# Maxima rows in the last quarter of the contraction rows, written by ScalarE; key blocks without fills; third query amid the first maxima

## The chip, the core and the metric

The kernel runs on one core of a Trainium2 chip. TensorE (PE) multiplies matrices from on-chip memory into PSUM, VectorE (DVE) reduces and combines, ScalarE (ACT) evaluates functions and copies, GpSimd (POOL) does small elementwise work, and SyncE (SP) issues most DMA transfers. Each engine works through its own queue in order and waits on semaphores. The metric is the time of one execution in microseconds (us), the median of several.

## The reference

Two layers act on x (4 batches, 512 positions, 128 channels) with a context of 154 keys per batch:

- Layer 0: x += tanh(g) * attention(layernorm(x), ctx), 16 heads of 8 channels, softmax over 154 keys. Then x += tanh(g) * FFN(layernorm(x)), a feed-forward part with activations rounded to 16 bits and weights to 4 bits.
- Layer 1: the same attention with its own weights and much larger keys, then a recurrent cell of four steps over the batches, which ends in a tanh.

What is computed for a head is softmax(q k / sqrt(8)) v for 512 queries and 154 keys. The kernel subtracts each query's largest score before the exponential; the masks of layer 1 only keep a tile's overlapping keys from counting twice.

## The kernel before

**Queries and key blocks.** `Q4` holds a batch's queries for scores with 128 contraction rows: of every four rows (`PARTS = 4`) one is the query's high part, one its low part, one the high part again, and the fourth is a row for maxima. `Kd` holds for every group of four heads four blocks of 154 keys; block j has keys only in 32 of the 128 rows, the rest is zero. One matmul thus gives the scores of three or four heads, or, with `Kd` as the stationary operand, the transposed scores of one head. There are three buffers of each, used in turn by batch number n = 4 * layer + b. All zeros are written by fills: VectorE and GpSimd fill `Q4` and `Kd` (`clear`, `clear_rest`, `clear_early`, `clear_late`), then engines copy 32 rows a block (`diagonal`).

**Maxima.** First pass, per batch: `scores_for_top` computes the scores in units (22 in layer 0, 20 in layer 1) of up to four heads into one of three PSUM banks (`MRING`), and VectorE's `take_top` reduces each to negative maxima. `split_top` splits them in high and low parts (`nms`), TensorE's `turn_top` transposes them into the PSUM bank `misc`, ScalarE's `copy_top` copies 32 rows into `nmT`, and SP's `tops` writes them by two DMAs into the maxima rows of `Q4`. The second pass (`scores`, 16 tiles of 128 keys and 4 tail tiles) then gives scores less the maximum, ScalarE's `exps` turns each tile, and TensorE's `weigh` multiplies them with the values in rounds of four tiles.

**Order.** Loops over layer, iteration i = -1 to 4 and slot 0 to 19 set every engine's queue: in iteration i slot s, score tile s of batch i is computed, and maxima units of batch i+1 in slots 0 to 12. Iteration -1 is a prologue: only the maxima units of batch 0. Some units are taken early, in slots 17 to 19 of the iteration before: for batch 1 eight (`FIRST_EARLY`). All else stands in plans of (slot, what, shift): "pre" is the transposing of a normalised batch, "q" its projection to queries, "top" the turning of maxima, "post" the transposing after attention, "wo" the projection of the output. Shift 3 stands for the third query in the prologue, shift -1 for the previous batch. "pre", "q", "top", "post" and "wo" share the one bank `misc`; `fill_misc` makes TensorE wait until the previous user has been read, which for the maxima is `nmT_r`.

**GpSimd's queue in layer 0** is: fills, the root of the first two norms, more fills, the frames of ones in the values (`frames`), `biases`, `values`, `tail_keys`, and then, in the loop, the third batch's norm, its key block and its low query part.

Of the kernel before, what the change touches and what calls it, by code (L numbers as in the profile page):

```python
# [32 lines left out]
PARTS = 4  # L33
# [6 lines left out]
FIRST_EARLY = 8  # L40
# [58 lines left out]
PE_PLAN = [(1, "tail0", -1), (3, "tail1", -1), (4, "pre", 2), (18, "pre", 3), (6, "q", 2), (19, "q", 3), (7, "round0", 0), (8, "wo", -1),  # L99
# [5 lines left out]
ACT_PLAN = [(5, "pre", 2), (6, "q", 2), (14, "top", 1), (18, "pre", 3), (19, "q", 3), (16, "post", -1),  # L105
# [12 lines left out]
VALUES_AT = ((0, -1, 5), (0, -1, 9))  # L118

# [61 lines left out]
def program(nc, x, w, wkr, ctxT, tailT, wffn, cols, rows, consts, masks, out):  # L181
    with ExitStack() as ctx:  # L182
# [61 lines left out]
        with ExitStack() as stretch:  # L244
# [11 lines left out]
            nmT = sb_here("nmT", [32, 2, T], F32R)  # L256
# [13 lines left out]
            nil = sb_here("nil", [32, T])  # L270
# [39 lines left out]
        q4_clear, kd_clear, nil_r = sem("q4_clear"), sem("kd_clear"), sem("nil_r")  # L310
        zero_r = sem("zero_r")
# [10 lines left out]
        m_in = [sem(f"m_in{n}") for n in range(3)]  # L322
# [25 lines left out]
        def misc_read(name):  # L348
# [8 lines left out]
            if kind == "top":  # L357
                return nmT_r, B * name[1] + name[2] + 1
# [16 lines left out]
        def q_landed(n):  # L375

            return q_in[n % 3], 16 * sum(5 if m in CLEAN_MAX_ROWS else 3 for m in range(n % 3, n + 1, 3))

        def kd_cleared(layer, b):

            return kd_clear, 3 if (layer, b) == (1, 0) else 2 * layer + min(b, 2) + 1
# [3 lines left out]
        def _(sp):  # L385
# [13 lines left out]
            def queries(layer, b):  # L399
                n = B * layer + b  # L400
                sp.wait_ge(q4_clear, 3 * layer + min(b, 2) + 1)
                if n >= 3:
                    sp.wait_ge(score_r, TILES * (n - 2))
                for a, (src, ready) in enumerate(((qh, qh_r), (ql, ql_r), (qh, qh_r))):
                    sp.wait_ge(ready, n + 1)
                    sp.dma_start(Q4[n % 3][a:P:PARTS, :, :].bitcast(F32),
                                 src[:, n % 2, :].bitcast(F32)).then_inc(q_in[n % 3], 16)
                if n in CLEAN_MAX_ROWS:
                    sp.wait_ge(nil_r, 1)
                    for a in range(2):  # L410
# [1153 lines left out]
```

## Time and profile before

| | us |
|---|---|
| runs | 371.2, 370.77, 369.09 (median 370.77) |
| profiled execution | 368.43 |
| its span, first to last instruction | 366.2 |
| busy in the span | PE 290.1, DVE 250.3, ACT 193.0, POOL 127.5 |
| granted TensorE clock, mean | 0.925 |

Two attention phases (20 to 128 us and 221 to 325 us) enclose the feed-forward part; the recurrent cell lies at the end. In each attention phase iteration -1 ends with the first score tile (48.4 and 241.7 us), and iterations 0 to 3 follow. Busy shares are means over stages with different limits, so each stage is read by itself. A line such as "PE L914" is line 914 of the kernel; the bracket at the end of a line of the timeline is the engine's idle time before it and what released it.

### The profile page before, as it was taken

The numbers are of one execution on the slowest core, as the hardware profiler recorded it, in microseconds if no ns is written. First come the engines' busy times: TensorE is split into PE (matmuls) and PEld (weight loads), VectorE is DVE, ScalarE is ACT, GpSimd is POOL, SyncE is SP. The second block draws the span as 40 slices with busy tenths as digits, with TensorE's granted clock in tenths as the row PEclk, the third lists the DMA queues.
The fourth block names the chain that finished last, engine by engine and source line by source line (L and its number), as shares of the span: only waits on it lengthen the run. The fifth ranks groups of instructions, "written<-read, shape, count | busy, mean of one in ns | idle before, by whom it ended". The sixth has DMA issues, their size and how long they took to land. (4 is left out here: it accounts for less than half of the span.)

```text
span 366.2 us, 4506 instructions
## 1 busy us (share of the span) xinstructions
PE 290.1 (79%) x1459; PEld 171.7 (47%) x1459; DVE 250.3 (68%) x530; ACT 193.0 (53%) x302; POOL 127.5 (35%) x263
## 2 busy tenths in 40 slices
PE   0976299899998785996006888899999999999794
PEld 0554164454543243431005765575665755544444
DVE  4788364896963589789989968765685792415414
ACT  1635066466466734869689634056555547463122
POOL 6588870444050301780001069431165023030300
PEclk9989689999999999998556999599999999999989
DMA  8721020020000000000000011110001000000004
GB/s 218 278 83 61 9 86 4 5 93 7 2 8 0 3 0 0 3 0 0 1 0 0 0 61 55 61 70 23 9 37 63 2 0 10 0 2 0 1 0 116
DMA packets 9687, 12.56 MB, mean 34 GB/s; under 512 B 896, under 2 KB 5376, under 8 KB 9664
## 3 DMA queue, kind: packets, MB, share of 16 engines
q1 hardware_dynamic: 9232, 11.80, 9.0%
q10 hardware_dynamic: 432, 0.47, 0.7%
q8 instruction: 12, 0.20, 0.2%
q14 instruction: 11, 0.09, 0.1%
HBM read 4.27 MB, written 1.05 MB: 15 GB/s over the span
## 5 line engine op out<-in xcount | busy, mean ns | idle before, releaser
L1215 DVE TENSOR_REDUCE sb_nm<-ps_top 128x3 f32<-128x462 f32 (+2 forms) x168 | 97.3, 627 | 41.4 <-PE ps_top L900 25.9
L721 ACT ACTIVATE sb_pr<-ps_score 128x512 f32<-128x512 f32 (+1 forms) x160 | 89.7, 584 | 61.8 <-PE ps_score L931 28.0
L900 PE MATMUL ps_top<-sb_Kd,sb_Q 128*128 128x462 f32 (+3 forms) x240 | 73.7, 384 | 7.3 <-DVE sb_nm L1215 3.2
L928 PE MATMUL ps_score<-sb_Q,sb_Kd 128*128 128x512 f32 x128 | 59.6, 477 | 3.9 <-ACT sb_pr L721 3.9
L589 POOL TENSOR_SCALAR sb_var<-sb_mv 128x4 f32<-128x4 f32 x16 | 5.3, 333 | 147.7 <-DVE sb_mv L1178 147.5
L900 PEld LDWEIGHTS ps_top<-sb_Kd,sb_Q 128*128 128x128 f32 x240 | 44.8, 206 | 22.3 <-DVE sb_nm L1215 13.2
L928 PEld LDWEIGHTS ps_score<-sb_Q,sb_Kd 128*128 128x128 f32 x128 | 23.9, 190 | 40.3 <-ACT sb_pr L721 31.3
L960 PE MATMUL ps_pv<-sb_pr,sb_V 128*32 128x512 f32 x256 | 34.1, 605 | 0.0
L606 POOL TENSOR_SCALAR sb_xn<-sb_xr,sb_nmean,sb_rstd 128x128 f32<-128x128 f32 x48 | 21.2, 455 | 1.3
L877 PE MATMUL ps_misc<-sb_consts,sb_xn 128*128 128x128 f32 x64 | 11.3, 304 | 12.7 <-POOL sb_xn L606 11.1
L1235 DVE STREAM_TRANSPOSE sb_oq<-ps_pv 128x512 f32<-128x512 f32 x16 | 10.7, 696 | 13.3 <-PE ps_pv L960 13.3
L591 POOL TENSOR_TENSOR sb_rstd<-sb_var,sb_half 128x4 f32<-128x4 f32 x16 | 16.6, 1040 | 1.3
L491 POOL CAST sb_Kd<-sb_K 32x616 fp32r<-32x616 f32 x20 | 13.9, 694 | 8.5 <-ACT sb_front L810 7.5
L936 PE MATMUL ps_score<-sb_Q,sb_KT 128*128 128x512 f32 (+1 forms) x32 | 14.6, 472 | 1.7 <-ACT sb_pr L721 1.7
L960 PE MATMUL ps_pv<-sb_pr,sb_VT 128*32 128x512 f32 (+1 forms) x128 | 14.9, 550 | 0.9 <-ACT sb_pr L721 0.9
L877 PEld LDWEIGHTS ps_misc<-sb_consts,sb_xn 128*128 128x128 f32 x64 | 7.8, 155 | 16.2 <-POOL sb_xn L606 12.6
L1175 DVE BATCH_NORM_STATS2 sb_stat<-sb_xr 128x6 f32<-128x128 f32 x64 | 13.9, 279 | 1.4 <-DMA sb_xr<-x 1.1
L1016 PE MATMUL ps_misc<-sb_consts,sb_amx 128*128 128x128 f32 x10 | 2.9, 383 | 14.9 <-DVE sb_amx L1276 14.2
L693 ACT ACTIVATE sb_xnT<-ps_misc 128x512 f32<-128x512 f32 x8 | 4.8, 596 | 18.1 <-PE ps_misc L877 18.1
L931 PE MATMUL ps_score<-sb_maskr,sb_identr 128*128 128x128 f32 x64 | 14.2, 222 | 0.0
L904 PE MATMUL ps_top<-sb_maskr,sb_identr 128*128 128x512 f32 (+3 forms) x48 | 13.8, 289 | 0.0
L700 ACT ACTIVATE sb_qh<-ps_misc,sb_cols 128x512 fp32r<-128x512 f32 x8 | 5.5, 688 | 15.8 <-PE ps_misc L883 15.8
(167 smaller groups left out, 545.5 us busy)
## 6 DMA issues: line engine op xcount, KB each, us to landing
sb_Q<-sb_qh SPq DMA_DIRECT2D x16, 256.0 KB, 2.3
sb_Q<-sb_ql SPq DMA_DIRECT2D x8, 256.0 KB, 2.3
sb_xr<-x SPq DMA_DIRECT2D x4, 256.0 KB, 7.6
out<-sb_xr SPq DMA_DIRECT2D x4, 256.0 KB, 2.4
sb_wsb<-w SPq DMA_DIRECT2D x1, 704.0 KB, 8.4
sb_wf<-wffn SPq DMA_DIRECT2D x1, 576.0 KB, 8.2
sb_wkr<-wkr SPq DMA_DIRECT2D x2, 256.0 KB, 7.1
sb_Q<-sb_nmT SPq DMA_DIRECT2D x16, 32.0 KB
```

The lines of the kernel that those rows point to most:

```text
L491: ins = pool.tensor_copy(Kd[n % 3][q, :, j, :], K4[q, :, b, :])
L591: pool.tensor_tensor(rstd[:, k % 4, :], var[:, k % 4, :], half[:, :], ALU.pow).then_inc(rstd_r, 1)
L606: ins = pool.tensor_scalar(xn[:, kind == "post", t, :], xr[:, TT * b + t, :], nmean[:, k % 4, t:t + 1], rstd[:, k % 4, t:t + 1], ALU.add, ...
L721: act.activation(pr[:, k % PRING, q0:T], score[k % SRING][:, q0:T], ACT.Exp, scale=SCALE).then_inc(exp_r, 1)
L877: ins = pe.transpose(misc[:, P * t:P * t + P], xn[:, kind == "post", t, :], ident[:, :])
L900: ins = pe.matmul(cols[:, c0:c1, :], Q4[n % 3][:, g, P * qt:P * qt + P], Kd[n % 3][:, g, j:j + c1 - c0, 0:keys], start=True, stop=not mask ...
L928: ins = pe.matmul(ps[:, :], Kd[n % 3][:, g, j, 0:P], Q4[n % 3][:, g, :], start=True, stop=(layer == 0), skip_group_check=True)
L931: ins = pe.matmul(ps[:, 0:P], identr[:, :], maskT, start=False, stop=True, skip_group_check=True)
L936: ins = pe.matmul(ps[:, q0:T], KT[:, b, t - H, :], Q4[n % 3][:, t - H, q0:T], start=True, stop=(layer == 0), skip_group_check=True)
L960: ins = pe.matmul(acc[32 * g:32 * g + 32, q0:T], lhs, pr[:, (TILES * n + t) % PRING, q0:T], start=(r in (0, 2)), stop=(r >= 4), skip_group ...
L1175: ins = dve.bn_stats(stat6[:, k % 4, t, :], xr[:, TT * b + t, :])
L1215: dve.tensor_reduce(nm[:, :, :].rearrange("p t h -> p (t h)")[:, f0:f0 + heads], top[k % MRING][:, 0:keys * heads].rearrange("p (h k) -> p ...
```

## The change

- The contraction rows are laid out anew: rows 0 to 95 hold the three query parts (every third row), rows 96 to 127 the maxima. ScalarE writes these straight from `misc` into `Q4`, one copy for each of four groups of heads, two at slot 14 and two at slot 15; `nmT`, its two DMAs and SP's `tops` are gone. TensorE turns the maxima with matmuls against the identity instead of transposes.
- The zeros of the maxima rows, which the first pass needs, are written by one DMA per query from a tile of zeros. The low query part is issued last.
- Key blocks and tails are written over all 128 rows, as the keys times a column of ones and zeros (`block_of[j]`). All fills of `Q4`, `Kd` and `KT` are gone.
- The third query's "pre" and "q" in the prologues move from slots 18 and 19 to 8 and 11, and in layer 0 its norm on GpSimd moves ahead of `biases` and `values`.
- Batch 1's early units are three instead of eight, at slot 14 of iteration -1.
- ScalarE's copies of the values, its block of batch 1 and the masks of layer 0 move from ahead of the loop into slots 5 and 9, 6, and 16 of iteration -1.

```diff
-PARTS = 4
+PARTS = 3
+MAX0 = 96
-FIRST_EARLY = 8
+FIRST_EARLY = 3
+FIRST_EARLY_AT = 14
 def units_at(layer, i, slot):
-    if slot >= SLOTS - EARLY and 0 < i + 2 < B:
+    if (i, slot) == (-1, FIRST_EARLY_AT):
+        taken += [(1, u) for u in range(FIRST_EARLY)]
+    if slot >= SLOTS - EARLY and 1 < i + 2 < B:
-PE_PLAN = [..., (18, "pre", 3), ..., (19, "q", 3), ...
+PE_PLAN = [..., (8, "pre", 3), ..., (11, "q", 3), ...
-ACT_PLAN = [(5, "pre", 2), (6, "q", 2), (14, "top", 1), (18, "pre", 3), (19, "q", 3), (16, "post", -1),
+ACT_PLAN = [(5, "pre", 2), (6, "q", 2), (14, "top0", 1), (15, "top1", 1), (8, "pre", 3), (11, "q", 3), (16, "post", -1),
 def misc_read(name):
-                return nmT_r, B * name[1] + name[2] + 1
+                return nmT_r, G * (B * name[1] + name[2] + 1)
 def queries(layer, b):          # SP
+                sp.wait_ge(nil_r, 1)
...
+                sp.dma_start(Q4[n % 3][MAX0:P, :, :].bitcast(F32), nil[:, :, :].to_broadcast([32, G, T])).then_inc(q_in[n % 3], 16)
+                for a, src, ready in ((0, qh, qh_r), (2, qh, qh_r), (1, ql, ql_r)):
-            def tops(layer, b):
 def diagonal(layer, b):         # POOL; ACT and DVE alike
-                    ins = pool.tensor_copy(Kd[n % 3][q, :, j, :], K4[q, :, b, :])
+                    ins = pool.tensor_scalar(Kd[n % 3][:, :, j, :], K4[:, :, b, :].bitcast(F32), block_of[j], 1.0,
+                                             ALU.mult, ALU.mult)
                 if layer == 0:                                    # POOL's queue
-                    clear_rest()
                     frames()
+                    normed("pre", 0, 2)
                     biases()
                     values(0)
                     tail_keys(0)
-                else:
-                    clear_late()
-            def copy_top(layer, b):
+            def copy_top(layer, b, groups):
                 act.wait_ge(misc_full, use["top", layer, b] + 1)
-                act.activation(nmT[:, n % 2, :], misc[0:32, :], ACT.Copy).then_inc(nmT_r, 1)
+                for g in groups:
+                    act.activation(Q4[n % 3][MAX0:P, g, :], misc[MAX0:P, :], ACT.Copy).then_inc(nmT_r, 1)
 def turn_top(layer, b):         # PE
-                    ins = pe.transpose(misc[0:32, P * t:P * t + P],
+                    ins = pe.matmul(misc[MAX0:P, P * t:P * t + P], nms[:, t, :, :, :]...,
+                                    ident[:, :], start=True, stop=True)
 def scores(layer, b, t):        # PE
-                if t == 0:
-                    pe.wait_ge(m_in[n % 3], 2 * 16 * (n // 3 + 1))
+                if t < G:
+                    pe.wait_ge(nmT_r, G * n + t + 1)
```

## Rows read from the trace of the kernel before

**Rows 1.** Busy time by stage (iteration -1 in part, 0 and 1; then layer 1).
```profile
core 0: us, PE busy (x) PEld busy (x) DVE busy (x) ACT busy (x) POOL busy (x), PEclk, DMA share, GB/s
...
36.00:45.20 9.20, 2.60 (x9) 1.78 (x7) 2.82 (x5) 0.59 (x1) 7.86 (x22) 0.69 0.02 9
...
48.40:65.90 17.50, 16.13 (x85) 8.64 (x83) 9.80 (x19) 12.24 (x23) 4.62 (x9) 0.99 0.13 49
65.90:89.30 23.40, 21.55 (x123) 11.61 (x122) 19.36 (x49) 13.71 (x26) 11.98 (x23) 1.00 0.10 40
...
234.60:241.70 7.10, 7.05 (x29) 5.80 (x30) 4.41 (x7) 1.18 (x2) 0.00 (x0) 0.64 0.02 9
```

**Rows 2.** Timeline, end of layer 0's prologue (start us, length us, what).
```profile
34.74 0.31 ACT L747 ACTIVATE sb_identr<-sb_consts 128x128 fp32r<-128x128 f32 x1
34.89 0.28 DVE L1228 TENSOR_TENSOR sb_nms<-sb_nm,sb_nms 128x64 fp32r<-128x64 f32 x1
34.96 0.43 ACT L749 ACTIVATE sb_maskr<-sb_cmask 128x288 fp32r<-128x288 f32 x1
...
35.23 1.04 PE L914 MATMUL ps_misc<-sb_consts,sb_nms 128*32 128x128 f32 x4 [1.54 <-DVE sb_nms L1228]
...
36.30 0.59 ACT L712 ACTIVATE sb_nmT<-ps_misc 32x512 fp32r<-32x512 f32 x1 [0.91 <-PE ps_misc L914]
...
39.03 2.61 POOL L504 CAST sb_KT<-sb_K 32x512 fp32r<-32x512 f32 x4
...
43.46 1.74 POOL L606 TENSOR_SCALAR sb_xn<-sb_xr,sb_nmean,sb_rstd 128x128 f32<-128x128 f32 x4
...
45.25 1.12 PE L877 MATMUL ps_misc<-sb_consts,sb_xn 128*128 128x128 f32 x4 [6.64 <-POOL sb_xn L606]
...
50.26 4.64 ACT L721 ACTIVATE sb_pr<-ps_score 128x512 f32<-128x512 f32 x8
```

**Rows 3.** Timeline, ScalarE at the end of layer 1's prologue.
```profile
235.72 0.59 ACT L712 ACTIVATE sb_nmT<-ps_misc 32x512 fp32r<-32x512 f32 x1 [6.97 <-PE ps_misc L914]
...
243.50 1.09 ACT L721 ACTIVATE sb_pr<-ps_score 128x512 f32<-128x512 f32 x2
```

**Rows 4.** Timeline of TensorE: score 17 of iteration 0; the output's projection.
```profile
62.97 0.50 PE L936 MATMUL ps_score<-sb_Q,sb_KT 128*128 128x512 f32 x1 [0.45 <-ACT sb_pr L721]
...
77.86 1.05 PE L969 MATMUL ps_misc<-sb_wsb,sb_oT 128*128 128x128 f32 x8
```

**Rows 5.** Timeline, maxima and post norm at slots 14 to 16 of iteration 1.
```profile
84.66 0.61 PE L914 MATMUL ps_misc<-sb_consts,sb_nms 128*32 128x128 f32 x4
...
85.31 0.59 ACT L712 ACTIVATE sb_nmT<-ps_misc 32x512 fp32r<-32x512 f32 x1
...
85.80 1.05 ACT L721 ACTIVATE sb_pr<-ps_score 128x512 f32<-128x512 f32 x2
...
86.04 0.63 PE L877 MATMUL ps_misc<-sb_consts,sb_xn 128*128 128x128 f32 x4 [0.24 <-ACT sb_nmT L712]
```

**Rows 6.** The page's costliest groups (busy, mean ns) and DMA issues (KB, us to landing).
```profile
L1215 DVE TENSOR_REDUCE sb_nm<-ps_top 128x3 f32<-128x462 f32 (+2 forms) x168 | 97.3, 627 | 41.4 <-PE ps_top L900 25.9
...
L606 POOL TENSOR_SCALAR sb_xn<-sb_xr,sb_nmean,sb_rstd 128x128 f32<-128x128 f32 x48 | 21.2, 455 | 1.3
...
L491 POOL CAST sb_Kd<-sb_K 32x616 fp32r<-32x616 f32 x20 | 13.9, 694 | 8.5 <-ACT sb_front L810 7.5
...
sb_Q<-sb_qh SPq DMA_DIRECT2D x16, 256.0 KB, 2.3
```

**Rows 7.** Iteration 0 of layer 0, the matmuls of line 900 alone.
```profile
48.40:65.90 17.50, 6.32 (x26) 4.86 (x26) 0.99 0.13 49
```

**Rows 8.** Timeline of TensorE in the feed-forward part.
```profile
146.07 1.96 PE L1098 MATMUL ps_score<-sb_front,sb_wfT 128*128 128x512 f32 x4 [1.90 <-DVE sb_front L1365]
...
163.69 1.88 PE L1098 MATMUL ps_pv<-sb_front,sb_wfT 128*128 128x512 f32 x4
167.88 3.62 PE L1098 MATMUL ps_score<-sb_front,sb_wfT 128*128 128x512 f32 x4 [2.31 <-ACT sb_uf L777]
```

More of the change, by code:

```diff
@@ L118 @@
 VALUES_AT = ((0, -1, 5), (0, -1, 9))
+FIRST_DIAGONAL_AT = (0, -1, 6)
+MASKS_AT = (0, -1, 16)
 KRING = 4
@@ L211, in program @@
         lowrow = consts_sb[:, P + 1:P + 2]
+        block_of = [consts_sb[:, P + 2 + j:P + 3 + j] for j in range(J)]
         cmask = sb("cmask", [P, 2 * P + 32])
@@ L375, in q_landed @@
         def q_landed(n):
-            return q_in[n % 3], 16 * sum(5 if m in CLEAN_MAX_ROWS else 3 for m in range(n % 3, n + 1, 3))
-        def kd_cleared(layer, b):
-            return kd_clear, 3 if (layer, b) == (1, 0) else 2 * layer + min(b, 2) + 1
+            return q_in[n % 3], 16 * 4 * (n // 3 + 1)
         @block.sync
@@ L663, in copy_k, with copy_v @@
                                scale=lowrow).then_inc(kh_r, 1)
-            def copy_v(layer):
+            def copy_v(layer, kinds):
                 if layer == 1:
                     act.wait_ge(v_r, 1)
-                for t in range(2):
+                for t in kinds:
                     act.wait_ge(vmm, 2 * layer + t + 1)
@@ L1213, in take_top @@
                 f0, heads, keys = UNITS[layer][u]
+                if u == 0 and k > 0:
+                    dve.wait_ge(nms_r, B * layer + b)
                 dve.wait_ge(top_r, k + 1)
@@ L1510, in constants @@
     own = (a % 32 >= OWN)[:, None]
-    low = (a % PARTS == 2)[:, None]
-    return tuple(np.concatenate(parts, axis=1).astype(np.float32) for parts in ((ident, own, low), (top, main, tail)))
+    low = ((a < MAX0) & (a % PARTS == 2))[:, None]
+    head = np.where(a < MAX0, a // PARTS // D, a % H // G)[:, None] == np.arange(J)[None, :]
+    return tuple(np.concatenate(parts, axis=1).astype(np.float32) for parts in ((ident, own, low, head), (top, main, tail)))
 def kernel(**inputs):
@@ L1524 @@
         turned.append(t[:, order] if name.endswith("Wq") else t)
-    wkr = np.zeros((C, 2, G, J, 32), np.float32)
-    bkr = np.ones((J, 32, 2, G), np.float32)
+    wkr = np.zeros((C, 2, G, P), np.float32)
+    bkr = np.zeros((P, 2, G), np.float32)
+    for g in range(G):
+        bkr[MAX0 + g::G, :, g] = 1.0
     for n in range(2):
@@ L1532 @@
         for part in range(3):
-            wkr[:, n, :, :, part::PARTS] = wk
-            bkr[:, part::PARTS, n, :] = bk.transpose(1, 2, 0)
+            wkr[:, n, :, part:MAX0:PARTS] = wk.reshape(C, G, J * D)
+            bkr[part:MAX0:PARTS, n, :] = bk.transpose(1, 2, 0).reshape(J * D, G)
     ctx = np.asarray(inputs["ctx_1024"]).transpose(2, 0, 1)
```

120 lines of the change are left out of this document (44 added, 76 removed).

## The prediction

> **What bounds the kernel now.** I read the busy time by stage first [rows 1]. In the attention iterations TensorE is busy 16.13 of 17.5 us and 21.55 of 23.4 us: they are paced by TensorE with ScalarE and VectorE close behind, whatever waits there lengthens the kernel. The two places where TensorE waits are the prologues. From 36.0 to 45.2 us it is busy only 2.60 of 9.2 us. The timeline says why [rows 2]: the third query's transposes stand in TensorE's queue at slot 18 and wait 6.64 us for GpSimd, which first does the values, then the tail keys (2.61 us from 39.03) and only then the normalisation at 43.46. The maxima of batch 0 were split by 35.17 and copied by 36.89, yet the first exponential starts at 50.26. In layer 1 there is no such wait (234.6 to 241.7 us is full, at 0.64 of the clock), only eight early maxima units and the third query stand between the copy at 235.72 and the exponential at 243.50 [rows 3].
>
> **Prologue of layer 0.** Gone: all fills of Q and Kd, the tails' fill, and the place of the third query behind values and tail keys. GpSimd then normalises batch 2 right after the frames, before any value; TensorE takes its transposes at slot 8 and its projection at slot 11, among 22 reduces of VectorE that pace this stretch. I charge 0.3 us for them (0 if VectorE always has three units ahead, 1.2 if TensorE runs at half clock there). Maxima split: 35.17 + 0.3 = 35.5. Turning them is no transpose any more but an fp32 matmul, which is issued as two instructions; the projection of the output does the same four products in 1.05 us [rows 4], where four transposes took 0.61 at full clock [rows 5] and 1.04 at half [rows 2]. So 1.05 to 1.8 us, I take 1.4: 36.9. Then four ScalarE copies instead of one. Two ScalarE instructions of 512 columns start 0.49 apart (85.31 and 85.80) and the last runs 0.59 [rows 5]: 3 x 0.49 + 0.59 = 2.1, so 39.0. Identity and masks, moved behind them, are 0.31 + 0.43 us [rows 2]. First exponential at 39.8 instead of 50.26: **-10.5 us** (-9.5 to -11.5). Late next: the values on GpSimd. Their first copy moves only little, so they end near 37; round 0 wants them at slot 7, near 45. The DMAs that carried the maxima were hidden behind the same 6.64 us; taking them away gains nothing of its own.
>
> GpSimd's diagonals now write 128 rows by a tensor-scalar instead of copying 32. That operation at 616 columns is not in the trace: below it lies the copy of 616 columns, 0.694 us; above it the 128-column tensor-scalar of 0.455 us scaled by width, 2.19 us [rows 6]. I take 1.1, nearer the row of equal width: 4.4 us for a block instead of 2.96. In layer 0 the tail keys end near 41, the third block near 45.5, its low query lands near 49, and its first unit is wanted at slot 17, near 54. Nothing. The GPSIMD Engine Reference of the Trainium skill, section 3.1, gives one-input bodies of few operations about 1.03 cycles an element at 1.2 GHz; an estimate from it is the copy's price, with which this trace's copy agrees (0.694 us for 616 columns). By the page the block would cost no more than now and the sum would not move; only the last rival would lose its chance.
>
> SP's queue: for each query it issues one 256 KB zero DMA and three query parts instead of three parts (and two small ones twice), the zeros ahead of the query's wait, so they land while SP waits for the query. The low part is now last, three issues in either order. 0 us; if the zeros came late, one landing of 2.3 us [rows 6], once a layer. VectorE's and ScalarE's blocks keep their width in columns and so their time: 0.
>
> **Iteration 0 of both layers.** Batch 1's early units fall from eight to three, so five move out of the prologue into slots 0 to 12. In layer 0, TensorE's unit matmuls are 6.32 us for 14 units in this iteration [rows 7], 0.45 each or 2.3 for five, of which TensorE's idle time of 1.4 us takes little; below, 0.5 if ScalarE hides them, above, five reduces of 0.627 us [rows 6], 3.1. I take **+2.0 us**. In layer 1 the five carry masks: **+2.2 us** (1 to 3.4).
>
> **The maxima copies at slots 14 and 15.** This is the term that decides. Iteration 1 now: TensorE turns the maxima at 84.66, ScalarE copies at 85.31, does exponentials 15 and 16 from 85.80, and TensorE's next user of the same PSUM bank, the transposes of the post norm at slot 16, starts at 86.04, as soon as the copy ends at 85.90 [rows 5]. Both queues are in order. After: the matmuls end 0.45 later; ScalarE copies two groups (85.75, 86.24), does exponential 15 (86.73), copies the other two (87.22, 87.71), done at 88.30. The post transposes wait for all four copies, since they overwrite the bank: they start at 88.44 instead of 86.04, **+2.4 us**. Behind them in TensorE's queue stand score 17, round 3 and the next early units, behind those VectorE's reduces; nothing of it can start earlier. It holds for iterations 1 and 2 of both layers: 4 x 2.4 = **+9.6 us**. Bounds for each: 0.45 (all but the dearer matmuls regained) and 3.4 (one more us at low clock). In iteration 0 no post norm follows; there exponential 15 is behind two more copies, round 3 and score 17 (62.97 now [rows 4]) wait for it: 63.9, +0.95, and the later copies keep that: 2 x 0.95 = **+1.9 us**.
>
> **Prologue of layer 1.** The copy begins at 235.72, after 1.04 us of turning as in layer 0, so the maxima are split near 234.6. The third query among the reduces adds 0.4, and the third early unit, which needs the last reduce's buffer, stands before the turn: 235.9. At half clock 1.8 us of matmuls, to 237.7; then the copies; exponential at 239.6 instead of 243.50 [rows 3]: **-3.9 us** (-2.5 to -5). GpSimd's fills there delay nobody: TensorE has no idle time in that stretch [rows 1]. Both first iterations now begin out of stretches granted 0.69 and 0.64 on the mean, partly at 1.2 GHz, where iteration 0 of layer 0 had 0.99 [rows 1]: **+1.0 us** in all (0 to 2).
>
> **Sum.** -10.5 + 2.0 - 3.9 + 2.2 + 9.6 + 1.9 + 1.0 = +2.3 us. The profiled execution took 368.43 us (366.2 of span, 2.2 around it), so 370.7; the median of the runs is 370.77, 2.3 above the profiled one, so on the median's basis 373.1 us. A measurement here tells 0.5%, 1.9 us, from no change.
>
> **Rivals.** (B) *The delays at the copies are regained*: VectorE, not TensorE, would pace the following slots. For: it is busy 19.36 of 23.4 us of iteration 1, with only 4.0 us idle [rows 1]. Against: its reduces come from units that stand behind the blocked transposes. If each of the four costs 0.5 instead of 2.4, the sum is 2.3 - 7.6 = -5.3 and the time 370.77 - 5.3 = 365.5 us: faster. It decides from 1.1 us regained of each 2.4, where the sum passes -1.9.
> (C) *The clock falls at each copy stall.* TensorE would stand 2.1 us at slot 16, four times. After an idle of 2.31 us in the feed-forward part, four matmuls took 3.62 us where four just before took 1.88 [rows 8]: 1.8 us each time, +7.2: 380 us. Against: four after an idle of 1.90 us took 1.96, full clock [rows 8]. [...]
> (D) *The five moved units are free*: iteration 0 is paced by ScalarE (12.24 busy) and they slip beside it: 2.3 - 3.7 = -1.4, 369.4 us.
> (E) *The tensor-scalar is at its upper bound*: 8.8 us a block and, scaled likewise, 7.2 for tail keys puts the third block of layer 0 at 53 and the low query's landing near 57, so slot 17 waits 3 us, and again 3 in iteration 1: 379 us. That is also the case in which the change does not do what it says, for GpSimd would still hold the queue.
>
> **How the numbers follow.** Forecast 0.42, B 0.22, C 0.14, D 0.13, E 0.09. The forecast's own range, 370.5 to 376, comes from the bounds of its terms taken against each other; 0.24 of it is beyond +0.5%, 0.16 within, 0.02 below. B gives 0.20 faster and 0.02 same; D 0.06 faster, 0.07 same; C all slower; E 0.08 slower, 0.01 same. Together faster 0.28, same 0.26, slower 0.46. The range reaches from the middle of B to the middle of C, leaving out 0.11 and 0.07: 365.5 to 380.
>
> **What would show it.** TensorE's gap before 45 us gone, first exponential near 40 (and 240 less the shift in layer 1). Post transposes at slot 16 with an idle of about 2 us released by the copy into Q, four times; iteration 1 lasting about 25.8 instead of 23.4 us: if it stays at 23.4, B is right. Iteration 0 at 20 to 21 us instead of 17.5: if 18, D. Full-clock matmuls right after the stall exclude C. GpSimd's block near 4.4 us decides E. Wrong altogether would be a stage outside the prologues and slots 14 to 16 that moves by over 1 us.

## The result, and the profile after

| | before | changed |
|---|---|---|
| runs, us | 368.73 to 371.2, median 369.93 | 380.51, 383.31, 382.93, 378.34, median 381.72 |
| ratio, 95% interval | | 1.030 (1.025 to 1.035) |
| profiled execution, its span | 368.43, 366.2 | 380.51, 378.7 |
| busy PE, DVE, ACT, POOL | 290.1, 250.3, 193.0, 127.5 | 297.2, 248.7, 207.7, 108.5 |
| granted clock, mean | 0.925 | 0.913 |

The change makes the kernel 3.0% slower. The forecast was 373.1 us, with 380 as the upper end of its range; the measured 381.7 lies beyond it. Medians and ratios, here and below, leave out executions over 1.5% above a kernel's fastest; with them the medians of experiments 2 (both edits), 3 (three units), 7 (first) and 8 (the turn) are 369.2, 370.2, 364.6 and 377.7 us, and the recorded expectations quote the first two.

The same stages as in [rows 1], in the changed kernel (start and end, length, busy time of PE, PEld, DVE, ACT and POOL with counts, granted clock, DMA share, GB/s):

```profile
36.00:42.80 6.80, 4.92 (x22) 2.85 (x22) 5.75 (x12) 3.96 (x9) 5.40 (x18) 1.00 0.29 80
40.90:61.60 20.70, 17.83 (x89) 10.19 (x89) 11.73 (x22) 14.25 (x28) 10.47 (x17) 0.92 0.05 14
61.60:88.60 27.00, 22.97 (x132) 12.70 (x131) 20.26 (x50) 16.48 (x30) 12.33 (x23) 1.00 0.15 39
234.60:244.20 9.60, 7.67 (x33) 4.46 (x34) 9.31 (x16) 3.42 (x6) 6.54 (x11) 1.00 0.60 160
```

TensorE's hole before 45 us is gone. Iteration 0 takes 20.7 us in place of 17.5 and iteration 1 takes 27.0 in place of 23.4; in the latter TensorE is idle for 4.0 us where it was for 1.9.

Next, ScalarE at the end of both prologues (answers to the last line of [rows 2] and to [rows 3]):

```profile
40.06 2.04 ACT L676 ACTIVATE sb_Q<-ps_misc 32x512 fp32r<-32x512 f32 x4 [1.55 <-PE ps_misc L881]
42.79 1.09 ACT L685 ACTIVATE sb_pr<-ps_score 128x512 f32<-128x512 f32 x2
...
243.30 2.04 ACT L676 ACTIVATE sb_Q<-ps_misc 32x512 fp32r<-32x512 f32 x4 [2.76 <-PE ps_misc L881]
245.37 1.09 ACT L685 ACTIVATE sb_pr<-ps_score 128x512 f32<-128x512 f32 x2
```

The first exponential moved from 50.26 to 42.79 us in layer 0, but from 243.50 to 245.37 in layer 1: all that layer 0's prologue had won is spent by then.

Slots 14 to 16 of iteration 1, as in [rows 5]:

```profile
81.18 1.06 PE L881 MATMUL ps_misc<-sb_consts,sb_nms 128*32 128x128 f32 x8
...
82.28 1.07 ACT L676 ACTIVATE sb_Q<-ps_misc 32x512 fp32r<-32x512 f32 x2 [0.53 <-PE ps_misc L881]
...
84.00 1.07 ACT L676 ACTIVATE sb_Q<-ps_misc 32x512 fp32r<-32x512 f32 x2
...
85.21 0.63 PE L844 MATMUL ps_misc<-sb_consts,sb_xn 128*128 128x128 f32 x4 [2.31 <-ACT sb_Q L676]
```

This is the forecast's picture: four copies, and the post transposes 2.31 us idle behind them. And the page's groups (busy, mean ns, idle time before and its releaser; for DMAs count, KB, us to landing), answering [rows 6]:

```profile
L844 PE MATMUL ps_misc<-sb_consts,sb_xn 128*128 128x128 f32 x64 | 10.6, 290 | 15.5 <-ACT sb_Q L676 9.1
...
L458 POOL TENSOR_SCALAR sb_Kd<-sb_K,sb_consts 128x616 fp32r<-128x616 f32 x20 | 15.8, 790 | 16.3 <-ACT sb_front L777 7.7
...
sb_Q<-sb_qh SPq DMA_DIRECT2D x16, 256.0 KB, 3.4
sb_Q<-sb_nil SPq DMA_DIRECT2D x8, 256.0 KB, 3.5
```

9.1 us of waiting for the copies; GpSimd's block at 0.79 us, 3.2 for four; and the high parts' landing at 3.4 us where it took 2.3 (the low part's is 3.0).

The time between the same events in both profiled executions shows where the 12.5 us of span came from (first units are line 900 before, 867 after; copies are the first copy of the maxima of each batch; post is ScalarE's copy of the post norm):

| stretch | before | after | difference | forecast |
|---|---|---|---|---|
| start to first unit, layer 0 | 20.05 | 23.02 | +3.0 | 0 |
| to first exponential | 30.21 | 19.77 | -10.4 | -10.5 |
| to copy of batch 1 | 11.61 | 14.76 | +3.15 | +2.0, and part of 1.0 for the clock |
| to copy of batch 2 | 23.44 | 24.73 | +1.3 | +0.95 |
| to copy of batch 3 | 21.83 | 24.46 | +2.6 | +2.4 |
| to post of batch 2 | 18.14 | 20.41 | +2.3 | +2.4 |
| to post of batch 3 | 17.69 | 17.85 | +0.2 | 0 |
| feed-forward, to first norm's copy of layer 1 | 71.44 | 73.32 | +1.9 | 0 |
| to first unit, layer 1 | 6.55 | 8.07 | +1.5 | 0 |
| to first exponential | 22.54 | 18.98 | -3.6 | -3.9 |
| to copy of batch 1 | 12.45 | 14.23 | +1.8 | +2.2, and part of 1.0 |
| to copy of batch 2 | 24.22 | 25.58 | +1.4 | +0.95 |
| to copy of batch 3 | 23.02 | 27.18 | +4.2 | +2.4 |
| to post of batch 2 | 22.53 | 27.47 | +4.9 | +2.4 |
| to post of batch 3 | 23.36 | 23.36 | 0 | 0 |
| to the end | 17.12 | 15.51 | -1.6 | 0 |

Three entries stand out: both first units (+4.5 together), and iterations 1 and 2 of layer 1 (4.3 above their terms). The clock explains the latter. Windows of the changed kernel: in and behind the copies' wait of iteration 1 of layer 1, behind that of iteration 2, and in and behind that of iteration 1 of layer 0:

```profile
286.00:288.00 2.00, 0.00 (x0) 0.00 (x0) 0.00 (x0) 1.93 (x5) 0.47 (x2) 1.00 0.00 0
...
290.00:292.00 2.00, 2.00 (x9) 0.34 (x6) 0.69 (x1) 0.00 (x0) 0.00 (x0) 0.50 0.00 0
...
318.00:320.00 2.00, 1.86 (x7) 1.58 (x7) 0.00 (x0) 0.98 (x2) 0.00 (x0) 0.50 0.00 0
320.00:322.00 2.00, 2.00 (x12) 0.55 (x10) 0.00 (x0) 1.19 (x2) 0.00 (x0) 0.50 0.00 0
...
83.00:85.20 2.20, 0.00 (x0) 0.02 (x1) 0.00 (x0) 2.13 (x5) 0.14 (x1) 1.00 0.00 0
85.20:88.00 2.80, 2.79 (x18) 1.57 (x19) 0.64 (x2) 1.83 (x4) 0.00 (x0) 1.00 0.00 0
```

In layer 1 TensorE runs at 0.50, its level of 1.2 GHz, after each stall; in layer 0, after a stall as long, it stays at 1.00 in this execution.

The clock is also behind 0.9 us of the first +3.15. The start of iteration 0 of layer 0, in the changed kernel and in experiment 1, whose code is the same up to there:

```profile
43.00:46.00 3.00, 2.47 (x8) 2.25 (x9) 1.19 (x2) 1.77 (x4) 2.63 (x5) 0.52 0.00 0
```
```profile
43.00:46.00 3.00, 2.26 (x11) 1.71 (x12) 1.58 (x3) 2.69 (x5) 2.63 (x5) 1.00 0.00 0
```

From first exponential to copy of batch 1 it is 14.76 us with the first and 13.89 with the second.

And the first query (SyncE's issues, then TensorE's first unit, then windows):

```profile
9.76 0.72 SPq L412 DMA_DIRECT2D sb_Q<-sb_nil  x1
...
17.01 0.55 SPq L415 DMA_DIRECT2D sb_Q<-sb_ql  x1
17.60 0.66 SPq L412 DMA_DIRECT2D sb_Q<-sb_nil  x1
...
23.02 2.24 PE L867 MATMUL ps_top<-sb_Kd,sb_Q 128*128 128x462 f32 x6 [5.26 <-DMA sb_Q<-sb_ql]
...
15.00:17.00 2.00, 1.03 (x4) 0.40 (x3) 2.00 (x7) 1.70 (x4) 1.62 (x12) 1.00 0.89 186
17.00:19.00 2.00, 0.63 (x4) 0.42 (x4) 1.97 (x5) 0.64 (x1) 0.66 (x5) 1.00 1.06 228
```

The last part is issued at 17.0 and its unit starts at 23.0, and the DMA engines are nearly full from 15 us on. Before, it was 2.4 us from the last issue (17.64) to the unit (20.05), and the same stretch showed a share of 0.18:

```profile
15.00:17.00 2.00, 2.00 (x8) 1.04 (x6) 2.00 (x7) 1.75 (x4) 0.00 (x0) 1.00 0.18 64
```

### The profile page after: what moved, and what is told of

The parts are those of the page before. It is cut to its first block and busy times, and to the rows that moved or that the text cites. A ratio compares the mean times of both kernels' runs of the same rounds, so it can differ in the third digit from the quotient of the medians.

```text
span 378.7 us, 4600 instructions
## 1 busy us (share of the span) xinstructions
PE 297.2 (78%) x1491; PEld 175.0 (46%) x1491; DVE 248.7 (66%) x529; ACT 207.7 (55%) x326; POOL 108.5 (29%) x252
## 5 line engine op out<-in xcount | busy, mean ns | idle before, releaser
L685 ACT ACTIVATE sb_pr<-ps_score 128x512 f32<-128x512 f32 (+1 forms) x160 | 90.8, 586 | 68.1 <-PE ps_score L898 31.1
L867 PE MATMUL ps_top<-sb_Kd,sb_Q 128*128 128x462 f32 (+3 forms) x240 | 72.9, 379 | 11.0 <-DMA sb_Q<-sb_ql 5.3
L895 PE MATMUL ps_score<-sb_Q,sb_Kd 128*128 128x512 f32 x128 | 60.4, 482 | 5.3 <-ACT sb_pr L685 3.8
L867 PEld LDWEIGHTS ps_top<-sb_Kd,sb_Q 128*128 128x128 f32 x240 | 43.9, 203 | 26.6 <-DVE sb_nm L1184 12.4
L927 PE MATMUL ps_pv<-sb_pr,sb_V 128*32 128x512 f32 x256 | 35.8, 632 | 0.0
L676 ACT ACTIVATE sb_Q<-ps_misc 32x512 fp32r<-32x512 f32 x32 | 17.0, 582 | 7.2 <-PE ps_misc L881 7.1
L458 POOL TENSOR_SCALAR sb_Kd<-sb_K,sb_consts 128x616 fp32r<-128x616 f32 x20 | 15.8, 790 | 16.3 <-ACT sb_front L777 7.7
L1142 DVE BATCH_NORM_STATS2 sb_stat<-sb_xr 128x6 f32<-128x128 f32 x64 | 13.9, 279 | 3.3 <-DMA sb_xr<-x 3.1
```

The lines of the kernel that those rows point to most:

```text
L458: ins = pool.tensor_scalar(Kd[n % 3][:, :, j, :], K4[:, :, b, :].bitcast(F32), block_of[j], 1.0, ALU.mult, ALU.mult)
L676: act.activation(Q4[n % 3][MAX0:P, g, :], misc[MAX0:P, :], ACT.Copy).then_inc(nmT_r, 1)
L685: act.activation(pr[:, k % PRING, q0:T], score[k % SRING][:, q0:T], ACT.Exp, scale=SCALE).then_inc(exp_r, 1)
L867: ins = pe.matmul(cols[:, c0:c1, :], Q4[n % 3][:, g, P * qt:P * qt + P], Kd[n % 3][:, g, j:j + c1 - c0, 0:keys], start=True, stop=not mask ...
L895: ins = pe.matmul(ps[:, :], Kd[n % 3][:, g, j, 0:P], Q4[n % 3][:, g, :], start=True, stop=(layer == 0), skip_group_check=True)
L927: ins = pe.matmul(acc[32 * g:32 * g + 32, q0:T], lhs, pr[:, (TILES * n + t) % PRING, q0:T], start=(r in (0, 2)), stop=(r >= 4), skip_group ...
```

## The experiments

Each is compared with the kernel before on the same chip; medians in us, ratios with 95% intervals. "Less" is the median against the changed kernel's 381.7, measured apart from them, and the kernel before has medians from 369.0 to 370.7 on these chips: a difference under some 2 us is not told by medians alone. "Profiled" means the interval between events as in the table above, in one execution. The edits are shown cut, without the waits and counts that go with them.

**1. The late transpose.**
```
 for at, what, shift in plan:
+    if what == "post" and at == 16 and i in (1, 2):
+        at = 18
```


> The changed kernel (381.7 us) with the transpose behind slot 16 and its copy put at slot 18 in iterations 1 and 2 of both layers; nothing else differs. Theory (the copies of the maxima hold the shared bank for 2.2 us four times, and in layer 1 TensorE's granted clock falls to 0.50 behind two of these stalls, which costs 2.0 and 2.7 us): the row that names TensorE's idle time before this transpose as waiting for the maxima copy falls from 9.1 us to under 1, the clock in the middle of layer 1 stays at 1.00, and the time falls by 8.8 to 13.5 us, to 368 to 373 us. Rival (waiting only; the low clock has another cause): the stalls go, a stretch at 0.50 remains, 373 us. Rival (ScalarE is the bound there, the two extra exponentials' worth of copies must be waited for wherever the transpose stands): the wait moves to a score behind slot 16, 380 us or more.

371.5, ratio 1.003 (1.000 to 1.006): 10.3 less. The clock stays at 1.00 in the middle of layer 1. There the two iterations with stalls are 27.18 and 27.47 → 24.52 and 24.02; in layer 0 only 24.46 and 20.41 → 23.62 and 19.65. TensorE's waits, the changed kernel first, then this one (total us, times, longest):

```profile
PE ps_misc L844 <- ACT sb_Q L676: 9.1, 4, 2.3
...
PE ps_score L903 <- ACT sb_pr L685: 3.0, 4, 1.1
```
```profile
PE ps_score L905 <- ACT sb_pr L687: 7.7, 10, 1.1
```

The wait at the bank is gone, but 4.7 us come back at the tail scores, which wait for exponentials that are behind the copies. In layer 0, where the changed kernel's clock did not fall, a stretch with a stall is thus shorter by 0.8 us only; in layer 1 the two are shorter by 2.7 and 3.5, and most of the difference is the clock.

**2. Zeros by memset, and both.**
```
-sp.dma_start(Q4[n % 3][MAX0:P, :, :], nil ...)
+if n >= 3: sp.dma_start(...)
+dve.memset(Q4[0][MAX0:P, :, :], 0.0)    # at the start
+pool.memset(Q4[1][MAX0:P, :, :], 0.0)   # at the start; Q4[2] behind the second norm
```


> The changed kernel with the maxima rows of the first three queries zeroed by memsets (VectorE for the first, GpSimd for the second and third) in place of SyncE's DMAs; queries 3 to 7 keep the DMA. Theory (the second query's zero DMA, issued 0.6 us behind the first query's last part, shares the DMA engines with it, so it lands 5.4 us after issue in place of 2.4): the first unit of layer 0 falls back from 23.0 to about 20.1 us, and the time falls by about 3.0 us, to 378.7. Rival (the new row layout itself, every third partition of 96, makes the transfer slow): the first unit stays at about 23 us and the time at 381.7. Rival (the memsets delay the first norms): first unit later than 23 us, 383.

378.7, ratio 1.022 (1.017 to 1.028): 3.0 less. The second norm is 1.2 us later behind the memsets, so the last part is issued at 18.24; its unit starts 3.1 us behind that, at 21.35, in place of 6.0. The four other profiles with these memsets have 3.1 too; the five others with both zero DMAs in place have 5.5 to 7.1, and their first unit at 22.3 to 23.7 us however early the part was issued (15.7 to 18.2).

> Both edits, the late transpose and the memsets for the first three queries, on the changed kernel. If the two costs are independent, the gains add: 3.0 + 8.8 to 13.5, that is 365 to 370 us, under or at the 369.9 of the kernel before. If one of them only exposes the other's wait, less than the sum: 371 us or more.

369.0, ratio 0.996 (0.993 to 0.999): the two gains add up, to the level of the kernel before.

**3. The schedule alone, on the kernel before.**
```
-(18, "pre", 3), (19, "q", 3)
+(8, "pre", 3), (11, "q", 3)
-FIRST_EARLY = 8        # at slots 17 to 19
+FIRST_EARLY = 3        # at slot 14
 frames()
+normed("pre", 0, 2)
 biases()
```
ScalarE's copies of the values, its block of batch 1 and the masks move into iteration -1 as in the change.

> The kernel before with only the schedule of the change: third query's transpose and projection at slots 8 and 11 of both prologues, its norm on GpSimd ahead of the biases, ScalarE's copies of values, first diagonal and masks in the plan, and three units of the second query at slot 14 in place of eight behind it. Maxima still go by DMA, key blocks still by fills and partition copies. Theory (the schedule part gains, the layout part loses): prologue of layer 0 -10.5, of layer 1 -3.9, moved units +2.0 and +2.2, so -10.2 us: 359.7. Rival (the time won in a prologue is lost later, because iteration 0 then waits for something that used to be hidden, such as the maxima DMAs or GpSimd): 366 us or more. Rival (no gain, the layout was needed for it): 369.9.

369.8, ratio 0.998 (0.995 to 1.001): no gain, where 359.7 was expected. The first exponential is at 44.73 in place of 50.26, but iteration 0 gives 2.9 us of it back, layer 1's prologue is no shorter (23.2 against 22.5), and its iteration 0 is 2.8 longer. The maxima's DMAs, which I had called hidden, are no longer so:

```profile
PE ps_score L938 <- DMA sb_Q<-sb_nmT: 3.6, 1, 3.6
```

That window is the end of layer 0's prologue; layer 1 has the same wait, 7.1 us in both. Behind it the granted clock is low, so that part of iteration 0's loss is the clock and not the moved units:

```profile
44.00:47.00 3.00, 3.00 (x10) 2.56 (x10) 1.45 (x3) 1.79 (x3) 2.75 (x5) 0.50 0.09 32
```

> The kernel before with the early third query as in the run of the schedule alone (370.2 us), but with eight units of the second query at slots 17 to 19 of the prologues, as before, in place of three at slot 14. Theory (the five units moved into iteration 0 cost what that run shows, 2.9 us in layer 0 and 2.8 in layer 1 between the first exponential and the maxima copy, while at the prologue's end they cost no more than the wait for the maxima DMA that covers them, 3.6 us twice): iteration 0 shrinks from 14.5 back to 11.6 us, the first exponential comes 1 to 2 us later, time 367 to 369. Rival (TensorE and VectorE do the same work either place, the sum doesn't change): 370.2. Rival (the units were what hid nothing, they come on top): 372 or more.

Only `FIRST_EARLY` is back at 8. 364.2, ratio 0.985 (0.981 to 0.989): 1.5% faster than before, and more than the 367 to 369 expected. ScalarE here:

```profile
40.21 0.59 ACT L716 ACTIVATE sb_nmT<-ps_misc 32x512 fp32r<-32x512 f32 x1 [1.06 <-PE ps_misc L921]
...
44.29 2.28 ACT L725 ACTIVATE sb_pr<-ps_score 128x512 f32<-128x512 f32 x4 [2.96 <-PE ps_score L935]
...
55.91 0.57 ACT L716 ACTIVATE sb_nmT<-ps_misc 32x512 fp32r<-32x512 f32 x1
```

Eight units fit whole into the DMA's 3.6 us, TensorE no longer waits there, and the exponential is not late by them; iteration 0 is 11.62 in place of 14.54, with the clock at 1.00 from 44 to 47 us. In layer 1 the prologue takes 1.0 more and iteration 0 2.8 less.

**4. Copies shared**, on the kernel with both edits.
```
-(14, "top0", 1), (15, "top1", 1)      # ScalarE
+(14, "top0", 1)                       # groups 0 and 1
+(14, "rows", 1)                       # VectorE
+dve.wait_ge(nmT_r, 2 * n + 1)
+for g in (2, 3): dve.tensor_copy(Q4[n % 3][MAX0:P, g, :], Q4[n % 3][MAX0:P, 0, :])
```


> The changed kernel with late transpose and memsets (369.2 us), and two of the four maxima copies made by VectorE from the rows that ScalarE has just written in SBUF, so ScalarE copies twice in place of four times per query. Theory (what is left of the cost, 1.3 to 1.8 us in each of iterations 1 to 3 of both layers, is ScalarE's time for three more copies than before, 0.58 us each, in stages where its exponentials set the pace): 1.2 us less in each of six iterations, 4 to 7 us in all, time 362 to 365. Rival (the copies lie beside other work once the transpose is late; the remaining cost is in the wait for the first group): under 1 us, 368.5. Rival (VectorE's reduces are now delayed in turn): 369.2 or more.

368.0, ratio 0.997 (0.994 to 1.000), against 0.996 without: the rival. The profiled iterations are as they were (24.76, 23.55 against 24.73, 23.63), the tail scores still wait 0.9 us on the mean, eight times. No cost of ScalarE's second pair of copies can be told once the transpose is late; what is left hangs on the first pair, between exponentials 14 and 15, or on the turn (experiment 8). These two were not told apart.

**5. The layout alone.**
```
-(8, "pre", 3), (11, "q", 3)
+(18, "pre", 3), (19, "q", 3)
-FIRST_EARLY = 3        # at slot 14
+FIRST_EARLY = 8        # at slots 17 to 19
```


> The changed kernel with the schedule of before: third query's transpose and projection at slots 18 and 19, eight units of the second query at slots 17 to 19. Only the row layout, the zero DMAs, the key blocks without fills and ScalarE's copies of the maxima are left of the change. Theory (schedule and layout are independent; the schedule alone was worth -0.4 us): 382 us. Rival (the direct copies only gain where the third query is early, since else the copies wait for TensorE anyway): 385 or more. Rival (the layout costs less with the old schedule, because the zero DMA of the third query falls elsewhere and the eight units cover the copies): 378 or less.

385.9, ratio 1.044 (1.039 to 1.048). By the ratios the layout part costs 4.4% with the old schedule and 3.2% with the new one (16 and 12 us): they are not independent. First unit to exponential is 23.3 us in layer 0 where the schedule and layout together have 19.8.

**6. TensorE kept busy in the stall.**
```
+if what == "post" and layer == 1 and i in (1, 2):
+    for _ in range(8):
+        pe.matmul(misc[0:96, 0:256], identr[:, 0:96], maskr[:, 0:256], ...)
```


> The changed kernel (381.7 us) with eight matmuls of 256 columns into the unused rows 0 to 95 of the shared bank put ahead of the transpose of iterations 1 and 2 of layer 1; they fill TensorE's wait for the maxima copies and compute nothing. Theory (the idle wait is what lowers the granted clock to 0.50 behind it): the wait stays as long, but the clock behind it stays at 1.00, and layer 1 is shorter by the 2.0 and 2.7 us (half of that if the fill does not cover the whole wait): 377 to 379.5. Rival (the clock falls there for another reason, such as the work ahead of the wait): the clock falls all the same, 381.7. Rival (the matmuls outlast the copies and delay the transpose): 382 or more.

377.6, ratio 1.024 (1.017 to 1.032): 4.1 less by medians, 2.1 by the ratios, whose intervals overlap, so the time alone does not settle it. The profile does. The transposes start 2.94 us behind the first copy in both kernels, but the clock holds:

```profile
285.00:287.00 2.00, 0.78 (x9) 0.58 (x7) 0.00 (x0) 1.92 (x4) 0.00 (x0) 1.00 0.00 0
287.00:289.00 2.00, 2.00 (x16) 0.80 (x13) 0.69 (x1) 0.98 (x2) 0.00 (x0) 1.00 0.00 0
...
311.00:313.00 2.00, 0.76 (x8) 0.70 (x8) 0.00 (x0) 1.66 (x5) 0.00 (x0) 1.00 0.00 0
313.00:315.00 2.00, 1.74 (x14) 0.74 (x12) 0.00 (x0) 1.40 (x4) 0.00 (x0) 1.00 0.00 0
```

The two iterations fall from 27.18 and 27.47 to 25.65 and 24.74: 4.3 us of low clock. In the same execution the first stall of layer 0, which is not filled, has the clock low behind it:

```profile
85.50:88.00 2.50, 2.50 (x11) 0.66 (x10) 0.64 (x1) 0.91 (x2) 0.00 (x0) 0.52 0.00 0
```

So filling the idle kept the clock up, in the one execution profiled; unfilled, the clock fell at these two stalls in 5 and 7 of 7 profiles (experiment 8).

**7. Where the moved units and the third query pay.** On the kernel of experiment 3 with eight units:
```
-(8, "pre", 3), (11, "q", 3)
+(18, "pre", 3), (19, "q", 3)   # at 8 and 11 in layer 0 only
```


> The kernel before with the early third query in layer 0 only (its place in layer 1 as before) and eight units at slots 17 to 19 in both layers; the run with it in both layers gave 364.2 us. Theory (in layer 1 the early third query lengthens the prologue, first unit to first exponential 24.2 us against 22.5 before, because its units share the stretch with it, and gains nothing later): 1.6 us less, 362.6. Rival (the 1.6 us come back in iteration 0 of layer 1): 364.2. Rival (layer 1's early query was worth something behind the prologue): 366.

364.3, ratio 0.981 (0.976 to 0.985), not to be told from 364.2. Layer 1's prologue is 1.65 us shorter, as expected, but the profiled layer 0, the same code, was 1.5 longer.

On the changed kernel, and on that of experiment 4:
```
-FIRST_EARLY = 3        # at slot 14
+FIRST_EARLY = 8        # at slots 17 to 19
```


> The changed kernel (381.7 us) with eight units of the second query at slots 17 to 19 of the prologues, as before, in place of three at slot 14; all else as changed. Theory (moving five units into iteration 0 costs 2.9 us there; what hides them at the prologue's end is the wait between the maxima's copy and the first score, which was 3.6 us with the DMA, but is only 0.6 to 0.9 us with the direct copies, so most of the eight units show there): iteration 0 -2.9, prologue +1.5 to +3, twice; time 379 to 382. Rival (as on the kernel before, -3 us per layer): 375.7.

380.4, ratio 1.027 (1.024 to 1.030): 1.3 less, which is no difference, within the theory. Profiled: prologues +0.5 and +2.7, iterations 0 -2.5 and -1.2; of the 2.5, 0.9 are the changed kernel's low clock there, so the five units cost 1.65 and 1.2 us in iteration 0.

> The changed kernel with all that has helped it: late transpose, memsets for the first three queries, copies shared with VectorE (368.0 us together), and now eight units at slots 17 to 19. By the same theory as the run before (exposed at the prologue's end): 366 to 368.5. Rival (-3 us per layer as on the kernel before): 362.

374.8, ratio 1.013 (1.008 to 1.017): 6.8 more than with three units, beyond both. From first unit to first exponential it is 3.7 and 4.0 us more, iterations 0 are 1.6 and 1.4 less; that is 4.7, and the profiled feed-forward part was 1.9 longer, of which below. Why the prologue of layer 0 loses 3.7 us here and 0.5 with four copies was not followed up; that two copies leave less to hide the units behind is an argument.

**8. The zero DMAs apart, and the turn.**
```
 sp.wait_ge(nil_r, 1)
+if n == 1: sp.wait_ge(*q_landed(0))
```


> The changed kernel with one wait more on SyncE: the second query's zero DMA is issued only once all four transfers of the first query have landed. Theory (that zero DMA, issued 0.6 us behind the first query's last part, is what holds it up; without it the part lands in 3.1 us as in the run with memsets, and the new row layout keeps 0.7 us of the delay): first unit at 20.1 to 20.5 us in place of 23.0, first exponential 2.5 to 3 us earlier, time 379. Rival (the transfer is slow by its layout, or by the first query's own zero DMA): first unit 23 us, 381.7. Rival (the second query now comes late, the wait moves to its units): first exponential earlier, iteration 0 longer, 381.7.

378.5, ratio 1.019 (1.013 to 1.024). The last part, issued at 17.42, has its unit at 22.25, not at 20.1 to 20.5 as expected: 4.8 us in place of 6.0. The second zero DMA is the lesser part. The median's fall of 3.2 us is more than these 1.2, and is left unexplained.

The other way round, `if n > 0` ahead of the zero DMA and a memset of `Q4[0]`:

> The changed kernel (381.7 us) with only the first query's maxima rows zeroed by VectorE's memset; the second's zero DMA stays 0.6 us behind the first query's last part. Theory (the first zero DMA, issued at 9.8 us while the inputs load, pushes the input traffic into the stretch from 15 to 17 us in which the query goes out, DMA share 0.89 there against 0.31 with memsets): first unit at 20.9 to 21.3 us in place of 23.0, exponentials 1.8 us earlier, time 380. Rival (the second zero DMA does it all): first unit 22.9 us, 381.7. Rival (memset on VectorE delays the first norm by as much as it saves): 22.5 us.

378.3, ratio 1.022 (1.017 to 1.028). Issued at 16.13, unit at 20.10: 4.0 us, 2.0 less than changed, where the first unit was expected at 20.9 to 21.3 (the last part was issued 0.9 earlier). The first unit with the second zero DMA held back, and with the first one gone:

```profile
22.25 2.24 PE L869 MATMUL ps_top<-sb_Kd,sb_Q 128*128 128x462 f32 x6 [4.32 <-DMA sb_Q<-sb_ql]
```
```profile
20.10 3.39 PE L869 MATMUL ps_top<-sb_Kd,sb_Q 128*128 128x462 f32 x9 [3.22 <-DMA sb_Q<-sb_ql]
```

The turn, with the maxima padded to 128 columns:
```
-pe.matmul(misc[MAX0:P, P * t:P * t + P], nms[:, t, ...], ident, ...)
+pe.transpose(misc[:, P * t:P * t + P], nmp[:, t, :], ident)
```

> The changed kernel with the maxima padded to 128 columns (96 zero columns, zeroed once at the start), so that four transposes turn them in place of eight matmul passes; nothing else differs. Theory (the turn took 1.06 us against 0.61 before, on the path from the last maximum to the copies): each of the eight queries 0.45 us shorter, 3.6 us in all, 378.1. Rival (the turn lies beside the exponentials, whose pace ScalarE sets at that point): 381 to 382. Rival (the wait for the copies takes it over in iterations 1 and 2, so only four queries gain): 380.

376.3, ratio 1.019 (1.013 to 1.025): 5.4 less, or 4.1 by the ratios; 3.6 was expected. The turn is four instructions again:

```profile
79.15 0.66 PE L882 MATMUL ps_misc<-sb_consts,sb_nmp 128*128 128x128 f32 x4
```

From first unit to the copy it is 0.5 and 0.3 less in the two layers, to the copies of batch 2 0.4 and 0.6 less: about the 0.4 that the turn is shorter. The other stretches differ by the clock, for in this execution it fell behind the first stall of layer 0 and the second of layer 1, where the changed kernel's fell behind both of layer 1. Layer 0, first stall:

```profile
80.00:83.00 3.00, 0.50 (x3) 0.26 (x2) 0.18 (x1) 2.93 (x6) 1.12 (x3) 0.92 0.00 0
83.00:86.00 3.00, 3.00 (x14) 1.20 (x13) 0.64 (x1) 1.34 (x3) 0.00 (x0) 0.51 0.00 0
```

Seven profiles have the four stalls unmended (the changed kernel, and experiments 2 without the late transpose, 5, 8 and the one with eight units). The clock fell behind 17 of their 28 stalls: 2 and 3 of 7 in layer 0, 5 and 7 of 7 in layer 1. Which ones differs from one execution to the next, and not by the length of the idle: the fourteen of layer 0 are 2.3 to 2.5 us, those of 2.31 us with both outcomes. Behind a late transpose it fell at none.

The edits of experiments 1, 2 and 4, the turn by transposes, and the zeros of layer 1:
```
-if n >= 3: sp.dma_start(Q4[n % 3][MAX0:P, :, :], nil ...)
+if n in (3, 7): sp.dma_start(...)
+pool.memset(Q4[n % 3][MAX0:P, :, :], 0.0)   # n = 4, 5, 6, behind the same waits
```


> The changed kernel with late transpose, copies shared with VectorE, maxima turned by transposes, and the maxima rows zeroed by memsets for queries 0 to 2 and 4 to 6 (those of the first two edits and the memsets of the first three queries gave 368.0 us together). Theory: the turns give up to 3.6 us, and in layer 1 the first unit comes 1.0 us behind the second norm's copy, as before, in place of 2.7, if the zero DMA is the cause: 362.8. Rival (the row layout, each transfer 3.1 us against 2.3 before, is the cause in layer 1): first unit still 1.8 us or more behind, 364. Rival (GpSimd's memsets at the layer's start hold up its norm of the third query): 368 or more.

366.5, ratio 0.989 (0.984 to 0.995): the best with the new layout, though above both 362.8 and the rival's 364. In layer 1 the first unit is still 2.58 us behind the second norm's copy (1.06 before, 2.58 changed), so there the zeros are innocent, as the rival said. The three query parts of that unit, which are all that the DMA engines move then (768 KB), in the kernel before and here:

```profile
218.20:220.50 2.30, 1.39 (x11) 0.95 (x9) 1.53 (x5) 0.60 (x1) 2.30 (x4) 1.00 0.88 342
```
```profile
218.80:222.10 3.30, 1.40 (x11) 0.96 (x9) 1.91 (x9) 0.60 (x1) 3.18 (x5) 1.00 0.95 238
```

The same bytes take 3.3 us in place of 2.3, with the engines as full: it is the new rows that make the transfer slower.

## Why the prediction was wrong

**Steps that held.** Layer 0's prologue from the first unit on: -10.5 forecast, -10.4 measured. Layer 1's: -3.9 against -3.6. In both some luck helped, for the turn starts later than the forecast had it (0.5 and 0.9 us, counted from the first unit) and takes 1.06 us at full clock in place of 1.4 and 1.8; and in layer 1 the forecast's own terms, 237.7 and 2.1 us of copies, give 239.8 and not the 239.6 that it used. The wait at slot 16: 4 x 2.4 forecast, 9.1 us in four waits measured. The copies of iteration 0: 0.95 against 1.3 and 1.4. The stretch with the moved units: 2.0 and 2.2 against 3.15 and 1.8. Of the 3.15, 0.9 are the low clock at the start, for which 1.0 was put down (seven other profiles with the same units and the clock at 1.00 have 13.6 to 13.9 us), and experiment 7 gives the units themselves 1.65 and 1.2 us; the rest comes with the layout. Rival D, in which they were free, is out. GpSimd's block, taken at 1.1 us, is 0.79: rival E is out. The prediction's estimate from section 3.1 of the GPSIMD Engine Reference in the Trainium skill, worked out with the page's own figures, is 616 x 1.03 / 1.2 GHz = 0.53 us, under the copy's 0.69 as well as this 0.79; that the trace agrees with it holds only roughly, and the measurements decide. Rival B is out, no stall was regained.

**The step that failed first** is "SP's queue ... 0 us; if the zeros came late, one landing of 2.3 us, once a layer". I looked at the zeros as something that might come late itself. They came early and made others late. From the issue of the first query's last part to its unit it is 2.4 us before and 6.0 changed; 4.0 without the first zero DMA (issued at 9.8 us, while the inputs load), 4.8 with the second held back, 3.1 with neither. So the two zero DMAs together cost 2.9 us (2.4 to 4.0 over six profiles), about 2.0 for the first and 1.2 for the second, each by one profile, and 0.7 is left. In layer 1, where no inputs load, taking the zeros away changed nothing (2.58 against 2.58 us from the norm's copy to the unit, 1.06 before). There the new rows, every third of 96, are the cause of 1.0 us: the three parts move at 238 GB/s in place of 342 (experiment 8). The other half of a microsecond lies between the end of the transfer and the unit, and its cause is open. The two first units make 4.5 us in all.

**The second** is the clock at the stalls: rival C, given 0.14. In the profiled execution it came at two of four stalls and cost 4.2 - 2.4 = 1.8 and 4.9 - 2.4 = 2.5 us; over seven profiles it came at 17 of 28; at two stalls with TensorE kept busy it did not. C put 1.8 us on each of four and so 380. The row after an idle of 2.31 us [rows 8] was the nearer one to a stall of 2.1 to 2.3 than the row after 1.90, and should have weighed more. Nor does the row after 1.90 us, which the forecast held against C, count against it: in the changed kernel the same four matmuls after the same idle take 2.96 us, not 1.96.

```profile
148.11 2.96 PE L1065 MATMUL ps_score<-sb_front,sb_wfT 128*128 128x512 f32 x4 [1.90 <-DVE sb_front L1334]
```

The sum on the profiled executions: 2.3 forecast, plus 3.0 + 1.5 for the landings, 4.3 for the clock in layer 1, 1.2 net for the other terms, most of them some tenths low, 0.3 for the feed-forward part and the end taken together (+1.9, -1.6), is 12.6; measured 12.5 of span. By the prediction's own sign, a stage outside the prologues and slots 14 to 16 that moves by over 1 us, the feed-forward part did so too.

**Right for part of the reason.** The stall at slot 16 is there as forecast, but it is not the shared bank alone that costs. Put behind it, the transpose starts freely, and two thirds of the stall stay in layer 0's iterations, as waits of the tail scores for exponentials: ScalarE's queue is what TensorE waits for there. That the DMAs that carried the maxima were hidden and taking them away gains nothing of its own was wrong too: with the third query early and only three early units they show, 3.6 us a layer, with a low clock behind the wait. So the direct copies did earn in the prologues of the change. With eight units the wait is filled, which is why the schedule alone gained nothing with three and 1.5% with eight.

**The feed-forward part** took 73.3 us, and its code did not change. Of the sixteen other profiles ten took 70.9 to 71.5 there, the kernel before with 71.4 among them, and six 72.5 to 74.4. The clock tells them apart: counted from ScalarE's copy of the post norm of batch 3, in the changed kernel and in these six it falls within the first nine microseconds of the part, in the ten it stays at 1.00 there. The same stretch, changed and before:

```profile
148.00:154.00 6.00, 5.89 (x10) 2.60 (x11) 3.20 (x6) 4.11 (x7) 3.19 (x5) 0.72 0.01 3
```
```profile
146.00:152.00 6.00, 5.92 (x14) 2.77 (x15) 4.26 (x8) 5.09 (x9) 3.36 (x7) 1.00 0.00 0
```

Six of the ten have the new layout too, so it does not force the low clock; but all four profiles with the old layout are among the ten, so that it makes it likelier is not ruled out.

**Open:** what decides at which of the stalls the clock falls, and why the layout costs more under the old schedule.

## What to carry to other kernels

A transfer that is early enough for its own reader can still be in the way of another's: price an added DMA by what else moves when it is issued. Work moved off a prologue is worth what it hid behind: here eight units fit for nothing under a 3.6 us landing, and made the prologues longer once that landing was gone (0.5 and 2.7 us with four copies, 3.7 and 4.0 with two). A stall of TensorE is to be priced twice, once for its length and once for the clock behind it; where it can't be removed, matmuls that compute nothing held the clock at both stalls where they were tried, worth 4.3 us in the profile.

## What the runs showed of the hardware that was not expected

- ScalarE's copy of 32 rows costs as much as one of 128: 0.58 us for 32x512 here, 0.60 for 128x512 in the kernel before.
- Eight records and 1.06 us for four fp32 matmuls of 128 columns, four and 0.66 for the same turn as transposes with 128 weight columns.
- Of stalls of 2.2 to 2.5 us, 17 of 28 were followed by a granted clock of 0.50 for some microseconds, each costing about 1.5 to 2.7 us. In layer 0, idles of the same 2.31 us had both outcomes.
- Three transfers of 256 KB from 128 rows into every fourth of 128 moved at 342 GB/s, into every third of 96 at 238 GB/s (layer 1, nothing else under way).
- GpSimd's tensor-scalar of 616 columns over 128 rows took 0.79 us against 0.69 for the copy over 32 rows.
